# Both operand sides of the distance product, and the means and variances of the later pairs, computed on GpSimd instead of VectorE

## What is computed

```python
def _L0_gnn_ref(x, mask, ...):                       # x is h = relu(layernorm(x)), mask is adj
    h = relu(bn1(conv1d(xc, conv1_w, 0)))            # 1 tap
    x_conv = relu(bn2(conv1d(h, conv2_w, 8)) + xc)   # 17 taps
    s = x @ w_se.T + b_se                            # 3 numbers per node
    sq = jnp.sum(s * s, axis=-1)
    dist = sq[:, :, None] + sq[:, None, :] - 2.0 * jnp.einsum('bnd,bmd->bnm', s, s)
    A = jnp.exp(-dist) * mask
    msg = relu(x @ w_msg.T + b_msg)
    x_nmp = jnp.einsum('bnm,bmd->bnd', A, msg)
    gi = concatenate([x_conv, x_nmp]) @ w_ih.T + b_ih
    gh = x @ w_hh.T + b_hh
    ... r, z, n gates ...
    return (1.0 - z) * nn_ + z * x
```

## Time and profile before

| | before |
|---|---|
| median of the runs | 320.89 us |
| profiled execution, device time | 321.41 us |
| its span on the core | 319.4 us |
| mean granted TensorE clock | 0.967 |
| PE busy | 292.3 us (92%) |
| PEld busy | 266.3 us (83%) |
| DVE busy | 255.6 us (80%) |
| ACT busy | 181.1 us (57%) |
| POOL busy | 21.9 us (7%) |

### The profile page before, as it was taken

The page is one execution under the profiler, slowest core; times in us unless marked ns, Lnnn a source line. Parts: engine busy times, 40 slices in busy tenths (PEclk is TensorE's granted clock), DMA queues, the critical chain, the costliest instruction groups (busy, mean ns, idle before and its releaser), DMA issues.

```text
span 319.4 us, 5823 instructions
## 1 busy us (share of the span) xinstructions
PE 292.3 (92%) x2025; PEld 266.3 (83%) x2025; DVE 255.6 (80%) x615; ACT 181.1 (57%) x332; POOL 21.9 (7%) x33
## 2 busy tenths in 40 slices
PE   5779677997999999999999999999999999999961
PEld 4579576787998899889998999899988999899860
DVE  5659997997989698978898698969897888673542
ACT  1575774599518953595529752995279545420530
POOL 6200300020002000200020000200020000000000
PEclk9587999999999999999999999999999999999995
DMA  5993029547049300941085205830292011001001
GB/s 92 255 223 67 1 58 209 130 121 143 2 95 185 112 8 29 218 118 34 2 183 135 78 2 120 168 110 0 61 205 67 0 30 37 3 0 56 12 10 56
DMA packets 28320, 27.45 MB, mean 86 GB/s; under 512 B 2532, under 2 KB 19956, under 8 KB 28164
## 3 DMA queue, kind: packets, MB, share of 16 engines
q1 hardware_dynamic: 27544, 26.75, 36.5%
q0 software_dynamic: 160, 0.07, 0.7%
q10 hardware_dynamic: 588, 0.27, 0.3%
HBM read 22.88 MB, written 4.19 MB: 85 GB/s over the span
## 4 chain that ended last, share of the span: by engine, by line
PE 81%; DVE 9%; DMA 3%; issue 3%; ACT 2%; SPq 1%; DVEq 0%; ACTq 0%
PE bank L1024 22%; PE bank L1025 22%; PE bank L1026 22%; PE bank L1133 4%; PE bank L1100 4%; DMA place<-in_L_gnn_conv_w 3%; PE bank L1195 3%; DVE w_lo L822 2%; PE bank L1078 1%; PE bank L1123 1%; PE bank L1208 1%; DVE place L829 1%; DVE adj_T L725 1%; PE bank L1110 1%; SPq L264 1%
## 5 line engine op out<-in xcount | busy, mean ns | idle before, releaser
L1024 PE MATMUL bank<-a_hi,w_hi 128*128 128x248 f32 (+2 forms) x328 | 94.5, 288 | 5.8 <-DVE w_lo L822 3.5
L1025 PE MATMUL bank<-a_lo,w_hi 128*128 128x248 f32 (+2 forms) x328 | 91.7, 280 | 0.0
L1026 PE MATMUL bank<-a_hi,w_lo 128*128 128x248 f32 (+2 forms) x328 | 91.7, 280 | 0.0
L1024 PEld LDWEIGHTS bank<-a_hi,w_hi 128*128 128x128 f32 x328 | 62.6, 191 | 7.3 <-issue 4.2
L1025 PEld LDWEIGHTS bank<-a_lo,w_hi 128*128 128x128 f32 x328 | 62.8, 191 | 0.6
L1026 PEld LDWEIGHTS bank<-a_hi,w_lo 128*128 128x128 f32 x328 | 62.6, 191 | 0.0
L1024 PE MATMUL bank<-h_hi,w_hi 128*128 128x512 f32 (+1 forms) x66 | 28.3, 429 | 2.8 <-DVE nmp_lo L735 1.5
L456 ACT ACTIVATE nmp_hi<-bank 128x512 fp32r<-128x512 f32 x16 | 9.5, 592 | 35.0 <-PE bank L1133 35.0
L335 POOL TENSOR_TENSOR rstd<-var_eps,halves 128x8 f32<-128x8 f32 (+1 forms) x9 | 14.4, 1595 | 211.2 <-DVE var_eps L637 211.2
L419 ACT ACTIVATE a_f<-bank,bn_shift,bn_scale 128x512 f32<-128x512 f32 x16 | 12.4, 777 | 24.4 <-PE bank L1026 24.4
L1025 PE MATMUL bank<-h_lo,w_hi 128*128 128x512 f32 (+1 forms) x66 | 26.2, 397 | 0.0
(11 more groups left out here) (147 smaller groups left out, 650.6 us busy)
## 6 DMA issues: line engine op xcount, KB each, us to landing
adj_in<-in_adj SPq DMA_DIRECT2D x64, 256.0 KB, 6.2
place<-in_x SPq DMA_DIRECT2D x32, 64.0 KB, 2.3
out<-x_slot SPq DMA_DIRECT2D x32, 64.0 KB
out<-place SPq DMA_DIRECT2D x32, 64.0 KB
x_slot<-in_x SPq DMA_DIRECT2D x28, 64.0 KB, 2.4
place<-in_L_gnn_conv_w SPq DMA_DIRECT2D x1, 1088.0 KB, 9.4
place<-in_L_gnn_w_ih SPq DMA_DIRECT2D x1, 384.0 KB, 7.2
x_slot<-in_x ACTq DMA_DIRECT2D x4, 64.0 KB, 2.7
```

Source lines behind the costliest of these rows:

```text
L1024: pe.matmul(out, w_hi[:, mat, :], hi, start=start, stop=False)
L1025: pe.matmul(out, w_hi[:, mat, :], lo, start=False, stop=False)
L1026: final = pe.matmul(out, w_lo[:, mat, :], hi, start=False, stop=stop)
```

## The change

`dist_sides` moves word for word from the DVE program to the POOL program, with one difference: the `tensor_reduce` over three squares becomes two additions with a wait between them, so it has 15 instructions. `x_moments` moves too, for pairs 1 to 7 (pair 0 keeps the DVE form in `first_pair`); there the fused last step becomes a multiplication by 0.25, a wait and an addition, so it has 8 instructions instead of 7. On POOL the order is `dist_sides(0)`, `x_moments(2)`, `norm_rstd(2)`, `dist_sides(1)`, and so on. `x_stats` on DVE gets a wait that keeps it from overwriting the statistics that POOL still reads. Nothing is moved on PE, ACT or SP.

```diff
+            def dist_sides(t):
+                e = ms_b[:, :, D:D + NSE]
+                pool.wait_ge(msb_ready, 3 * (t + 1))
+                wait(pool, distT_done, t)
+                pool.tensor_tensor(s_sq[:, :, :], e, e, ALU.mult).then_inc(ssq_ready, 1)
+                pool.tensor_copy(emb[:, :, 0:NSE], e).then_inc(emb_ready, 1)
+                pool.wait_ge(ssq_ready, t + 1)
+                pool.tensor_tensor(emb[:, :, NSE], s_sq[:, :, 0], s_sq[:, :, 1], ALU.add).then_inc(sq_part_ready, 1)
+                pool.wait_ge(sq_part_ready, t + 1)
+                pool.tensor_tensor(emb[:, :, NSE], emb[:, :, NSE], s_sq[:, :, 2], ALU.add).then_inc(emb_ready, 1)
...
+            def x_moments(i):
+                graphs, done = slice(0, PB), PB * i
+                pool.wait_ge(stats_ready, done)
...
+                pool.wait_ge(parts2_ready, 2 * (i + 1))
+                pool.tensor_scalar(diff_sq[:, graphs], diff_sq[:, graphs], 0.25, None, ALU.mult).then_inc(quarter_ready, 1)
+                pool.wait_ge(quarter_ready, i - 1)
+                pool.tensor_tensor(var_eps[:, graphs], diff_sq[:, graphs], sq_mean[:, graphs], ALU.add
+                                   ).then_inc(vareps_ready, 1)
...
-            for t in range(1, NP):
-                norm_rstd(t + 1, slice(0, PB))
+            pool.wait_ge(dve_const, DVE_CONSTS)
+            for t in range(NP):
+                dist_sides(t)
+                if t + 1 < NP:
+                    x_moments(t + 2)
+                    norm_rstd(t + 2, slice(0, PB))
...
             def x_stats(s, k):
                 dve.wait_ge(x_in[s % 4][k], x_count(s))
+                wait(dve, parts_ready, 3 * (s + 1) if s > 1 else 0)
...
-                dist_sides(0)
                 weights_low("a")
                 x_stats(1, 0)
                 x_stats(1, 1)
-                x_moments(2, 2 * PB, slice(0, PB))
...
                 if ahead:
                     messages(t)
-                    dist_sides(t)
                 common_part(s)
```

More of the change, by code:

```diff
@@ L175, in gnn_block @@
         msg_done, msb_ready, msg_ready = sem("msg_done"), sem("msb_ready"), sem("msg_ready")
+        sq_part_ready, quarter_ready = sem("sq_part_ready"), sem("quarter_ready")
         ssq_ready, emb_ready, part_ready, rest_ready, dist_in_ready = (sem(n) for n in (
@@ L242, in gnn_block @@
         DIST_OPS = 3 + 3 + 1
+        DVE_CONSTS = 7 + 1 + 3
         MSG_PARTS = ((0, 3), (3, 6), (6, 8))
@@ L340, in norm_rstd @@
                                    ).then_inc(nbias_ready, 1)
+            def dist_sides(t):
[8 more added lines that the diff above has]
+                pool.tensor_tensor(emb[:, :, NSE], emb[:, :, NSE], s_sq[:, :, 2], ALU.add).then_inc(emb_ready, 1)
+                pool.wait_ge(emb_ready, 2 * (t + 1))
+                pool.tensor_copy(emb_part[:, :, 0, :], emb[:, :, :]).then_inc(part_ready, 1)
+                pool.wait_ge(part_ready, 3 * t + 1)
+                pool.tensor_tensor(emb_rest[:, :, :], emb[:, :, :], emb_part[:, :, 0, :], ALU.subtract
+                                  ).then_inc(rest_ready, 1)
+                pool.tensor_copy(dist_l[:, :, 0:3 * EMB].rearrange("n b (k e) -> n b k e", k=3),
+                                emb_part[:, :, 0:1, :].broadcast_to([N, PB, 3, EMB])).then_inc(dist_in_ready, 1)
+                pool.wait_ge(rest_ready, t + 1)
+                pool.tensor_copy(emb_part[:, :, 1, :], emb_rest[:, :, :]).then_inc(part_ready, 1)
+                pool.wait_ge(part_ready, 3 * t + 2)
+                pool.tensor_tensor(emb_part[:, :, 2, :], emb_rest[:, :, :], emb_part[:, :, 1, :], ALU.subtract
+                                  ).then_inc(part_ready, 1)
+                pool.tensor_copy(dist_l[:, :, 3 * EMB:5 * EMB].rearrange("n b (k e) -> n b k e", k=2),
+                                emb_part[:, :, 1:2, :].broadcast_to([N, PB, 2, EMB])).then_inc(dist_in_ready, 1)
+                right = dist_r[:, :, 0:6 * EMB].rearrange("n b (k e) -> n b k e", k=6)
+                pool.tensor_scalar(right[:, :, 3:5, 0:NSE], emb_part[:, :, 0:2, 0:NSE], 2.0, None, ALU.mult
+                                  ).then_inc(dist_in_ready, 1)
+                pool.tensor_scalar(right[:, :, 5, 0:NSE], emb_part[:, :, 0, 0:NSE], 2.0, None, ALU.mult
+                                  ).then_inc(dist_in_ready, 1)
+                pool.wait_ge(part_ready, 3 * (t + 1))
+                pool.tensor_copy(dist_l[:, :, 5 * EMB:6 * EMB], emb_part[:, :, 2, :]).then_inc(dist_in_ready, 1)
+                pool.tensor_scalar(right[:, :, 0:3, 0:NSE], emb_part[:, :, :, 0:NSE], 2.0, None, ALU.mult
+                                  ).then_inc(dist_in_ready, 1)
+                pool.tensor_scalar(dist_r[:, :, ONE_SLOT:ONE_SLOT + 3], emb_part[:, :, :, NSE], -1.0, None, ALU.mult
+                                  ).then_inc(dist_in_ready, 1)
@@ new lines, in x_moments @@
+            def x_moments(i):
+                graphs, done = slice(0, PB), PB * i
+                pool.wait_ge(stats_ready, done)
+                wait(pool, xnorm_ready, done - graphs.stop)
+                even, odd = stats[:, graphs, 1], stats[:, graphs, 4]
+                pool.tensor_tensor(halves_sum[:, graphs], even, odd, ALU.add).then_inc(parts_ready, 1)
+                pool.tensor_tensor(halves_diff[:, graphs], even, odd, ALU.subtract).then_inc(parts_ready, 1)
+                pool.tensor_tensor(sq_sum[:, graphs], stats[:, graphs, 2], stats[:, graphs, 5], ALU.add
+                                  ).then_inc(parts_ready, 1)
+                pool.wait_ge(parts_ready, 3 * (i + 1))
+                pool.tensor_tensor(diff_sq[:, graphs], halves_diff[:, graphs], halves_diff[:, graphs], ALU.mult
+                                  ).then_inc(parts2_ready, 1)
+                pool.tensor_scalar(sq_mean[:, graphs], sq_sum[:, graphs], 1.0 / D, EPS, ALU.mult, ALU.add
+                                  ).then_inc(parts2_ready, 1)
+                pool.tensor_scalar(neg_mean[:, graphs], halves_sum[:, graphs], -0.5, None, ALU.mult).then_inc(mean_ready, 1)
+                pool.wait_ge(parts2_ready, 2 * (i + 1))
[3 more added lines that the diff above has]
+                                   ).then_inc(vareps_ready, 1)
@@ L614, in _ @@
                     dve.memset(dist_r[:, :, k * EMB + NSE], -1.0).then_inc(dve_const, 1)
-            DVE_CONSTS = 7 + 1 + 3
             def x_stats(s, k):
                 dve.wait_ge(x_in[s % 4][k], x_count(s))
+                wait(dve, parts_ready, 3 * (s + 1) if s > 1 else 0)
                 for b in range(k * GB, (k + 1) * GB):
@@ L686, in messages @@
                                       ).then_inc(msb_ready, 1)
[L688 to L720, removed]
@@ L929, in first_pair @@
                 conv_low(0, 1)
-                dist_sides(1)
                 phase_sums(1)
@@ L933, in first_pair @@
                 x_stats(2, 1)
-                x_moments(3, 3 * PB, slice(0, PB))
                 n_hidden(0, 0)
@@ L988, in iteration @@
                     x_stats(s + 2, 1)
-                    x_moments(s + 3, PB * (s + 3), slice(0, PB))
                 conv_out(s, 1, 0)
```

## The result

The change makes the kernel slower: 332.46 us (median of four runs, 332.32 to 333.76) against 320.86 us for the kernel before, run beside it. The ratio is 1.0368, with a 95% interval of 1.0341 to 1.0396. The profiled execution has a span of 330.1 us, 10.7 us over the 319.4 of before.

What follows compares the result with a forecast made beforehand. PE was taken to bound the long middle and DVE the start. Six waits of 1.3 us (7.8) less 0.5 at the start added 7.3 to 320.89, giving 328.2 us; the 8-in-10 range was 319.9 to 335.5 us.

Steps and rivals of the forecast that it cites:

- The step in the middle: Distance transposes, six iterations: POOL's dist_sides, 3.6 us at middle price, ends late; PE waits about 1.3 us each, 7.8 us.
- The step of the start: First pair: relief of DVE against slower moments on POOL, -0.5 us, with -1.4 and +1.0 as ends.
- What bounds the kernel: DVE sets the start, PE alone the long middle; there DVE time is worth nothing and PE waits add one for one.
- L746 and what follows: Middle: relieved DVE starts common_part (L746) near 151.1 instead of 151.80, then both L756 and the four sums.
- One POOL instruction per DVE instruction: Under back-to-back DVE instructions with two SBUF operands, POOL gets about one instruction done per DVE instruction.
- the end of the chain: dist_sides on POOL in an iteration: six openings for seven remaining instructions, the last after that, end at 154.9.
- the 1.4 us to be regained: Start, ahead of product "a0": 1.4 us of PE's 2.27 us wait for w_lo regained by relieving DVE.
- the second brake: Start: ACT makes weights_high("a0") only behind the copies of the distance transposes, so not all the time comes back.
- Moments in the middle: Eight POOL instructions for 0.84 us, some 1.5 to 3 us later, under 3.8 us of cover before ACT: cost 0.
- The fast one: Rival: POOL's pace near the low end or several instructions per opening; no middle wait, 319.5 us; chance 0.15.
- Every instruction costs 0.35 or more: Rival: every POOL instruction costs 0.35 us or more, wait 2.2 to 2.8 us, 336 us; chance 0.21.
- The late moments: Rival: POOL's power or bias late, ACT normalises late, PE's h_transposes after; 1 us an iteration, 334 us; chance 0.05.

Runs made afterwards that it cites:

- the sides alone: Changed kernel with x_moments of all pairs back on VectorE, only dist_sides on GpSimd: 331.88 us, ratio 1.0326 to the kernel before.
- moving the transposes: Changed kernel with PE's distance transposes behind all of product a0 and the output transposes, distances behind product b, in iterations 1 to 6: 322.0 us.
- the moments alone: Changed kernel with dist_sides back on VectorE, only the moments of pairs 1 to 7 on GpSimd: 324.16 us, ratio 1.0068 to the kernel before.
- the quiet run: Changed kernel with VectorE stopped behind common_part until GpSimd has finished the distance sides, iterations 1 to 6: 322.8 us.
- both kernels with an extra instruction: Changed kernel with one VectorE instruction added directly behind messages, iterations 1 to 6: two SBUF operands 341.23 us, one SBUF operand 333.04 us.
- the kernel with the two-operand instruction: Changed kernel with a VectorE addition of two constant SBUF operands, 512 columns, added directly behind messages in iterations 1 to 6: 341.23 us.

## Why the prediction was right, and where it was off

It forecast 328.2 us, slower, with a range to 335.5; measured were 332.46. The step in the middle held in kind and was too small in size: the wait of 1.67 us lies in the band of 0.6 to 1.9 that the forecast named, the time half a microsecond above its band of 324 to 332. The step of the start had the wrong sign.

- **What bounds the kernel.** Held. DVE lost 17 us of busy time and nothing came of it in the middle; six waits at the distance transposes carry the loss (10.8 us), the sides alone give the same six, and moving the transposes removes them but for one of 0.5.
- **L746 and what follows.** Held to 0.1 us: the residuals begin 1.79 us behind `messages` (155.46 - 153.67), as the sum had it, and the eighth POOL instruction ends 0.1 us later.
- **One POOL instruction per DVE instruction.** Held for `dist_sides`: six openings, six instructions, one left. It did not hold for the moments, as said below.
- **The mis-sized term is the end of the chain.** The sum let POOL finish 4.84 us behind `messages`, 0.1 us behind DVE's last sum. It took 5.36. Of these 0.52 us, 0.13 come ahead of the last opening (DVE's last sum, L729, ended 4.87 us behind `messages` instead of 4.74) and 0.39 behind it: L375 does 0.27 us of its own work after its opening (72 elements, 0.41 us long when free), and L377 ends another 0.22 later. The sum had allowed 0.1 for both. PE is late by all of it: the idle time of 1.67 us is counted from the modelled end of its last matmul, but from start to start the step into the transposes grew from 0.11 us (153.54 to 153.65) to 1.94 (157.15 to 159.09), and iterations are 36.09 - 34.27 = 1.82 us longer, not 1.3. Six times 0.5 us are 3 of the 4.3 us that the forecast misses; 0.7 lie in the start and 0.45 in the first iteration.
- **The start.** Forecast -0.5, with +1.0 at the other end; measured +0.21 (31.25 against 31.04). The term that failed is the 1.4 us to be regained ahead of product "a0". The wait there did go, from 2.27 us to 0.21, but PE now waits earlier, for POOL, at the distance transposes of pair 0, which the sum had left out. The timeline of PE of the changed kernel, first transpose and start of "a0":

```profile
31.95 0.23 PE L1133 MATMUL bank<-ident_b,dist_l 128*128 128x128 bf16 x1 [1.91 <-POOL dist_r L377]
...
35.95 0.36 PE L1047 MATMUL bank<-a_hi,w_hi 128*128 128x256 f32 x1 [0.21 <-issue]
```

  So "a0" begins 35.95 - 23.74 = 12.21 us behind product "g", and 36.62 - 24.42 = 12.20 before: nothing is regained. That "a0" began before 36.6, which was to speak for the step, is luck; the input transfers ended 0.68 us earlier in this execution. Either half alone does regain time there (11.58 us with the sides, 11.37 with the moments). In the whole start the sides alone gain 0.61 us and the moments alone cost 1.13, since the power then falls under two-operand work. In the changed kernel it didn't (1.67 us); there the first of the moments, which could begin only behind `dist_sides(0)`, took 1.12 us from 31.84, and the bias 0.56. The step had the second brake right: ACT makes the weights of "a0" only behind the copies of the distance transposes, which now come at 32.38, 8.64 us behind "g" instead of 6.58. The timelines of ACT and DVE of the changed kernel:

```profile
32.38 1.58 ACT L506 ACTIVATE dist_lT<-bank 32x256 bf16<-32x256 bf16 x4 [2.83 <-PE bank L1133]
```

```profile
35.03 0.82 DVE L851 TENSOR_TENSOR w_lo<-place,w_hi 128x640 fp32r<-128x640 f32 x1 [1.47 <-ACT w_hi L437]
```

  DVE is rid of 2.7 us of work and gives 1.47 of them back in this one wait.
- **Moments in the middle.** The result held, the cover did not quite. Moments alone leave the iteration at 34.27 us. But POOL takes 7.2 us from the first of the moments to the end of the bias (131.16 to 138.36 in that run), where it was 2.97 before (130.39 to 133.36): 4.2 us later, not 1.5 to 3. One instruction for each opening was too generous here. In each of the five iterations the negated mean (L394), 8 columns of one operand and 0.24 us long when free, outlasts both instructions of a pair; the timelines of POOL and DVE of the changed kernel:

```profile
135.25 1.40 POOL L394 TENSOR_SCALAR neg_mean<-halves_sum 128x8 f32<-128x8 f32 x1
```

```profile
135.28 1.27 DVE L806 SCALAR_TENSOR_TENSOR conv_lo<-place,conv_hi 128x512 fp32r<-128x512 f32 x2
```

  And ACT does wait for the bias. The first normalisation of one iteration on the timeline of ACT, moments alone and then the changed kernel:

```profile
138.39 1.65 ACT L450 ACTIVATE x_norm<-x_slot,norm_bias,rstd 128x128 f32<-128x128 f32 x4 [0.75 <-POOL norm_bias L341]
```

```profile
141.30 0.88 ACT L451 ACTIVATE x_norm<-x_slot,norm_bias,rstd 128x128 f32<-128x128 f32 x2 [0.76 <-POOL norm_bias L341]
```

  The 3.8 us of cover are overrun by up to 0.8 us; in each of the two kernels ACT loses 3.8 us so in five waits. None of it reached PE, whose waits for `x_norm` from 78 us on stay at a single one of 0.2 us in both, as before. So ACT has slack ahead of the transposes that read `x_norm`, which the sum had not counted.
- **Rivals.** The fast one is refuted by the pace, 0.23 us a piece when free, and by the openings. "Every instruction costs 0.35 or more" is refuted by the quiet run: 3.62 us for fifteen, almost the middle price of 3.6. When free, two-input instructions took 0.21 us for 8 elements and 0.25 for 32 (L351 and L364 of the quiet run). The late moments cost PE nothing in the iterations of the changed kernel; in three other profiled executions the late bias of pair 2 did, as told at the end.
- **The rule of the Trainium skill** (page "SBUF — State Buffer", section "Who interferes with whom") that the two engines shut each other out is borne out on POOL's side by both added and removed neighbours. On DVE's side the trace shows small losses, not whole waits: the pair L785 lasts 1.35 instead of 1.29 us, L722 0.45 instead of 0.42. That they grow was a sign of being wrong in the prediction; 0.03 to 0.06 us do not bear that out.

Does it add up? The first iteration, from the gate product to the distance transposes, is 2.27 us longer (31.92 against 29.65), the five others 1.82 each (9.1), the start 0.21, and the input transfers end 0.68 earlier (23.74 against 24.42): 10.9, where the spans differ by 10.7. The profiled executions differ by 10.9 in their whole time (332.3 against 321.4), and the medians by 11.6, since that of before lay 0.55 above its median and that of after 0.14 below.

## What to carry to other kernels

What the moved work costs on GpSimd depended here on what VectorE ran beside it (3.62 us alone, 5.28 beside two-operand work): price it once alone and once under the two-operand instructions that VectorE will run at that very time, for the relieved VectorE gets to them sooner. Look first whether the relieved engine holds anybody up, and how long the in-order engine behind the moved chain can wait: here 3.59 us of cover met a chain of 5.36, and an order on TensorE that asks 2 us later hid it, but for one wait of 0.5 us. Count also the first time that the chain runs: the start lost its gain to the same wait at pair 0.

## What the runs showed of the hardware

- **POOL can be passed over for a whole run of VectorE instructions.** Over the pair L806 this happens in each of the five iterations (1.40 us, shown above), in every kernel with the moments on POOL. Over a longer run it comes and goes. In the profiled execution with VectorE kept quiet, one `norm_bias` (free length 0.20) took 3.22 us; beside it DVE ran four two-operand instructions without a gap, the last of which ends at 70.84:

```profile
67.69 3.22 POOL L341 TENSOR_TENSOR norm_bias<-neg_mean,rstd 128x8 f32<-128x8 f32 x1
```

```profile
67.50 1.30 DVE L760 TENSOR_TENSOR edge_m<-adj_T,edge_m 128x512 f32<-128x512 f32 x2
68.70 0.70 DVE L838 TENSOR_TENSOR place<-place 128x512 f32<-128x512 f32 x1
69.30 1.54 DVE L734 TENSOR_TENSOR a_lo<-a_f,a_hi 128x1320 fp32r<-128x1320 f32 x1
```

  In the profiled execution of the changed kernel the same instruction met the same neighbours (it began at 67.08, DVE's pair at 66.92) and was through in 0.58 us. With VectorE kept quiet PE waited 2.99 us for the normalisation of pair 2, and its granted clock then fell to 0.57 from 76 to 80. The profiled executions of both kernels with an extra instruction show the same: 3.23 us for `norm_bias`, a wait of 3.0 us on PE. The execution that shows the event took 325.22 us, where the median of that kernel is 322.8. Why it gets an opening once and not another time was not settled, and no run tested it. It may be behind part of the spread of these kernels' times, but that is only argued.
- **The granted clock fell behind some of PE's waits of 2 us and more, and their length alone does not tell which.** Its lowest windows of 2 us were at 0.50 to 0.54 behind the six waits of 2.96 to 3.63 us that were read (three in the first pair, three for the normalisation of pair 2), and at 0.50 to 0.53 behind three of the six waits of 2.1 to 2.2 us in the kernel with the two-operand instruction. It was also at 0.50 from 26 to 28 in the kernel before, behind a wait of 2.19 us that ended at 24.42. It stayed at 1.00 behind the other three, behind all of 1.67 us, and behind those of 2.27, 2.34, 2.44 and 2.45 us. Where it fell in the middle of the kernel, 1.5 us were lost on top of the wait.
